# Softmax attention in a four-block network: row maxima of four heads turned and copied together

## The reference

```python
q = embedded @ Wq.T + bq; k = ...; v = ...          # 16 heads of 8 features
qk = jnp.einsum('bhqd,bhkd->bhqk', q, k) / sqrt(s)
p = jax.nn.softmax(qk, axis=-1)                      # over all 1024 keys
p = p * jnp.triu(ones((s, s)))                       # mask after the softmax
z = jnp.einsum('bhqk,bhkd->bhqd', p, v)
out = layernorm(embedded + z) * gamma + beta
```

## Time and profile before

| | us |
|---|---|
| median of 3 runs | 989.38 (987.41 to 995.13) |
| span of the profiled execution | 985.3 |
| soft stage, from the first A to the last B | 430 to 859 of the span |

### The profile page before, as it was taken

One profiled execution on the slowest core, in us unless ns is written; L12 is line 12 of the kernel. 1 busy time (PEld: TensorE's weight loads), 2 busy tenths in 40 slices (PEclk: granted clock), 3 DMA queues, 4 the chain that ended last, 5 costly groups with the idle time before them and its releaser, 6 DMA issues.

```text
span 985.3 us, 13757 instructions
## 1 busy us (share of the span) xinstructions
PE 675.3 (69%) x4446; PEld 334.1 (34%) x4446; DVE 582.2 (59%) x1035; ACT 443.7 (45%) x836; POOL 302.9 (31%) x679
## 2 busy tenths in 40 slices
PE   4042867332240992579999999999999999840694
PEld 4031322131230991213343423242323433230693
DVE  5216699760450345677878777767977777062243
ACT  2021500011210652405878676766667777720462
POOL 0605154414425341003242323141322323105242
PEclk9996889555655896757999999998999999965697
DMA  9942000002213101560030202030020000000203
GB/s 232 274 144 40 1 1 0 0 9 60 71 17 90 30 27 44 123 147 7 1 50 2 50 1 50 1 48 4 11 40 2 1 2 1 1 1 33 81 26 96
DMA packets 45926, 44.89 MB, mean 46 GB/s; under 512 B 5904, under 2 KB 36316, under 8 KB 45600
## 3 DMA queue, kind: packets, MB, share of 16 engines
q1 hardware_dynamic: 41168, 35.90, 15.6%
q0 software_dynamic: 4544, 7.60, 2.9%
q10 hardware_dynamic: 144, 0.51, 0.2%
HBM read 27.85 MB, written 17.60 MB: 46 GB/s over the span
## 4 chain that ended last, share of the span: by engine, by line
PE 51%; DVE 11%; issue 5%; DMA 5%; POOL 5%; ACT 3%; SPq 1%; POOLq 0%; ACTq 0%; DVEq 0%
PE PS L828 14%; PE PS L795 12%; PE PS L770 11%; PE PS L629 5%; PE PS L640 4%; POOL slots_x L1395 3%; DVE ARENA L1348 3%; ACT ARENA L987 2%; DMA ARENA<-slots_x 1%; POOL ARENA L1409 1%; DVE XN L1042 1%; PE PS L536 1%; DMA ARENA<-k_parts 1%; DVE STATS L1019 1%; DVE X L1086 1%
## 5 line engine op out<-in xcount | busy, mean ns | idle before, releaser
L1348 DVE TENSOR_REDUCE ARENA<-PS 128x1 f32<-128x1024 f32 x256 | 302.9, 1219 | 94.6 <-PE PS L770 94.1
L987 ACT ACTIVATE ARENA<-PS 128x512 f32<-128x512 f32 x512 | 279.6, 597 | 95.6 <-PE PS L795 89.2
L795 PE MATMUL PS<-ARENA 75*128 75x512 bf16 x512 | 174.9, 388 | 8.3 <-ACT ARENA L987 6.8
L770 PE MATMUL PS<-ARENA 72*128 72x512 bf16 x512 | 164.3, 406 | 21.3 <-DMA ARENA<-k_parts 16.9
L828 PE MATMUL PS<-ARENA 128*8 128x128 f32 (+8 forms) x1920 | 153.4, 435 | 0.7 <-ACT ARENA L987 0.7
L1460 POOL TENSOR_SCALAR_AFFINE_SELECT ARENA<-ARENA 128x128 f32<-128x128 f32 x256 | 74.6, 296 | 160.5 <-ACT ARENA L987 160.3
L581 PE MATMUL PS<-C,ARENA 128*128 128x128 f32 x78 | 17.1, 368 | 119.5 <-DMA ARENA<-slots_x 119.5
L1272 DVE TENSOR_TENSOR ARENA<-PS,ARENA 128x512 f32<-128x512 f32 x46 | 31.8, 692 | 96.3 <-PE PS L629 96.3
L554 PE MATMUL PS<-C,XN 128*128 128x128 f32 x96 | 24.1, 401 | 92.4 <-DVE XN L1042 88.8
L795 PEld LDWEIGHTS PS<-ARENA 75*128 75x128 bf16 x512 | 47.5, 98 | 105.5 <-ACT ARENA L987 56.5
L770 PEld LDWEIGHTS PS<-ARENA 72*128 72x128 bf16 x512 | 44.8, 100 | 104.1 <-issue 37.3
(11 more groups left out here) (130 smaller groups left out, 785.0 us busy)
## 6 DMA issues: line engine op xcount, KB each, us to landing
ARENA<-q_parts SPq DMA_DIRECT2D x24, 192.0 KB
ARENA<-k_parts SPq DMA_DIRECT2D x72, 64.0 KB
ARENA<-pack_dram SPq DMA_DIRECT2D x8, 514.0 KB
slots_x<-FILL SPq DMA_DIRECT2D x2, 1483.5 KB, 19.0
ARENA<-slots_x SPq DMA_DIRECT2D x10, 258.0 KB, 4.4
ARENA<-slots_x SPq DMA_DIRECT2D x8, 256.0 KB, 3.6
slots_y<-ARENA SPq DMA_DIRECT2D x16, 128.0 KB, 1.8
ARENA<-tokens_y SPq DMA_DIRECT2D x8, 256.0 KB, 3.7
```

What stands on the lines that cost most here:

```text
L770: ins = nc.tensor.matmul(PS[:, slot + c, :], Q3[0:KQ, G % Q3R, g, i * P:(i + 1) * P], K3[0:KQ, G % Q3R, g, c * 512:(c + 1) * 512], start=T ...
L795: nc.tensor.matmul(PS[:, bank, 0:w], K3[0:MR + 3, G % Q3R, i, j * P:(j + 1) * P], Q3[0:MR + 3, G % Q3R, i, half * 512:half * 512 + w], sta ...
L987: nc.scalar.activation(PT[:, n % NPT, 0:w], PS[:, 4 + ring_number[x] % NBB, 0:w], ACT.Exp).then_inc(b_exp, 1)
L1348: nc.vector.tensor_reduce(NM[:, k % 4, i:i + 1], PS[:, slot:slot + 2, :].rearrange("p b n -> p (b n)"), AX.X, ALU.max, negate=True).then_i ...
```

## The change

The unit of the maxima becomes one half of all four heads. The buffers `NM`, `NMR`, `M3` and `MT` hold 16 maxima columns (48 after the split) for each half, in two buffers where there were four. S, M and the copy are done once per half for four heads: 16 of each where there were 64. SP still issues 64 stores of the same size, now four behind each copy. PE waits at the first B of a half for all four (`m_rows[half]`, 64 counts per group). The planner's `LEAD` goes from 0 to 3: at a half's first B, three more turns must lie ahead beyond the M.

```diff
-LEAD = 0
+LEAD = 3
+MW = 4 * HQ
...
-        last = (hh, h)
+        last = (hh // 4, h) if hh % 4 == 3 else None
...
-    ahead = turns.index(("M", 3, 0)) + 1 + LEAD
+    ahead = turns.index(("M", 0, 0)) + 1 + LEAD
...
-                want = max(want, turns.index(("M", 4 * G + 3, s // TB)) + 1 + LEAD)
+                want = max(want, turns.index(("M", G, s // TB)) + 1 + LEAD)
...
-                        sp.wait_ge(m_copied, maxima_number[hh, h] + 1)
-                        sp.dma_start(Q3[MR:MR + 3, G % Q3R, g, tiles[0] * P:(tiles[-1] + 1) * P],
-                                     MT[0:3 * len(tiles), hh % 4, :]).then_inc(m_rows[hh % 4], 16)
+                        sp.wait_ge(m_copied, maxima_number[G, h] + 1)
+                        for g in range(4):
+                            sp.dma_start(Q3[MR:MR + 3, G % Q3R, g, tiles[0] * P:(tiles[-1] + 1) * P],
+                                         MT[3 * HQ * g:3 * HQ * (g + 1), h, :]).then_inc(m_rows[h], 16)
...
-                        at, width = unit_columns(i)
-                        o = PS[0:width, bank, 0:P // 2].bitcast(BF16)
-                        nc.tensor.transpose(o, M3[:, k % 4, at:at + width], IDB[:, :]).then_inc(m_turned, 1)
+                        o = PS[0:3 * MW, bank, 0:P // 2].bitcast(BF16)
+                        nc.tensor.transpose(o, M3[:, i, :], IDB[:, :]).then_inc(m_turned, 1)
...
-                            pe.wait_ge(m_rows[i], rows_stored(4 * G + i, half))
+                            pe.wait_ge(m_rows[half], 64 * (G + 1))
...
-                        nc.scalar.copy(MT[0:width, k % 4, :],
-                                       PS[0:width, 4 + ring_number[x] % NBB, 0:P // 2].bitcast(BF16)
+                        nc.scalar.copy(MT[0:3 * MW, i, :],
+                                       PS[0:3 * MW, 4 + ring_number[x] % NBB, 0:P // 2].bitcast(BF16)
                                        ).then_inc(m_copied, 1)
...
-                        nm, rest = NM[:, k % 4, tiles[0]:tiles[-1] + 1], NMR[:, k % 4, tiles[0]:tiles[-1] + 1]
-                        m0, m1, m2 = (M3[:, k % 4, at + r * n:at + (r + 1) * n] for r in range(3))
+                        nm, rest = (a[:, i, :].rearrange("p (g n) -> p g n", g=4) for a in (NM, NMR))
+                        m0, m1, m2 = (M3[:, i, :].rearrange("p (g r n) -> p g r n", g=4, r=3)[:, :, r, :]
+                                      for r in range(3))
```

More of the change, by code:

```diff
@@ L163, in macaron_kernel @@
         FILL = sb("FILL", [P, P + 1])
-        MT = sb("MT", [P, 4, P], BF16)
+        MT = sb("MT", [P, 2, P], BF16)
         B2 = sb("B2", [P, E * P])
@@ L252, in macaron_kernel @@
         ONE8 = m(32)
-        NM = m(4 * TB).rearrange("p (r i) -> p r i", r=4)
-        NMR = m(4 * TB).rearrange("p (r i) -> p r i", r=4)
-        M3 = m.bf(4 * 3 * TB).rearrange("p (r c) -> p r c", r=4)
+        NM = m(2 * MW).rearrange("p (r c) -> p r c", r=2)
+        NMR = m(2 * MW).rearrange("p (r c) -> p r c", r=2)
+        M3 = m.bf(2 * 3 * MW).rearrange("p (r c) -> p r c", r=2)
         RD = m(32).rearrange("p (c g) -> p c g", g=4)
@@ L355, in macaron_kernel @@
         m_copied = sem("m_copied")
-        m_rows = [sem(f"m_rows{k}") for k in range(4)]
+        m_rows = [sem(f"m_rows{k}") for k in range(2)]
         b_scores = sem("b_scores")
@@ L395, in macaron_kernel @@
         last_scores = {}
[L396 to L405, removed]
+        for G, h in maxima:
+            last_scores[G, h] = score_number["A", 4 * G + 3, tiles_of_unit(h)[-1]]
         turn_number = {x: n for n, x in enumerate(turns)}
@@ L413, in columns @@
             return 4 * P, (P * (j - HQ) if j >= HQ else None)
-        def unit_columns(h):
-            return 3 * HQ * h, 3 * HQ
         def masked_before(m):
@@ L500, in soft @@
                     if x[0] == "M":
-                        _, hh, h = x
-                        G, g = divmod(hh, 4)
+                        _, G, h = x
                         tiles = tiles_of_unit(h)
-                        sp.wait_ge(m_copied, maxima_number[hh, h] + 1)
-                        sp.dma_start(Q3[MR:MR + 3, G % Q3R, g, tiles[0] * P:(tiles[-1] + 1) * P],
-                                     MT[0:3 * len(tiles), hh % 4, :]).then_inc(m_rows[hh % 4], 16)
+                        sp.wait_ge(m_copied, maxima_number[G, h] + 1)
+                        for g in range(4):
+                            sp.dma_start(Q3[MR:MR + 3, G % Q3R, g, tiles[0] * P:(tiles[-1] + 1) * P],
+                                         MT[3 * HQ * g:3 * HQ * (g + 1), h, :]).then_inc(m_rows[h], 16)
                     if x[0] == "V" and x[1] % NS == NS - 1:
@@ L965, in soft @@
                         act.wait_ge(m_turned, maxima_number[k, i] + 1)
[L966 to L969, removed]
-                        nc.scalar.copy(MT[0:width, k % 4, :],
-                                       PS[0:width, 4 + ring_number[x] % NBB, 0:P // 2].bitcast(BF16)
+                        if k >= 1:
+                            act.wait_ge(m_rows[i], 64 * k)
+                        nc.scalar.copy(MT[0:3 * MW, i, :],
+                                       PS[0:3 * MW, 4 + ring_number[x] % NBB, 0:P // 2].bitcast(BF16)
                                        ).then_inc(m_copied, 1)
@@ L1344, in soft @@
                         dve.wait_ge(a_scores, score_number[x] + 1)
-                        if k >= 4 and i == 0:
-                            dve.wait_ge(m_split, last_unit(k - 4) + 1)
-                        nc.vector.tensor_reduce(NM[:, k % 4, i:i + 1],
+                        G, g = divmod(k, 4)
+                        h, it = divmod(i, HQ)
+                        if G >= 1 and g == 0 and it == 0:
+                            dve.wait_ge(m_split, maxima_number[G - 1, h] + 1)
+                        nc.vector.tensor_reduce(NM[:, h, HQ * g + it:HQ * g + it + 1],
                                                 PS[:, slot:slot + 2, :].rearrange("p b n -> p (b n)"),
@@ L1443, in soft @@
                         pool.wait_ge(a_max, last_scores[k, i] + 1)
[L1444 to L1447, removed]
-                        nm, rest = NM[:, k % 4, tiles[0]:tiles[-1] + 1], NMR[:, k % 4, tiles[0]:tiles[-1] + 1]
-                        m0, m1, m2 = (M3[:, k % 4, at + r * n:at + (r + 1) * n] for r in range(3))
+                        if k >= 1:
+                            pool.wait_ge(m_turned, maxima_number[k - 1, i] + 1)
+                        nm, rest = (a[:, i, :].rearrange("p (g n) -> p g n", g=4) for a in (NM, NMR))
+                        m0, m1, m2 = (M3[:, i, :].rearrange("p (g r n) -> p g r n", g=4, r=3)[:, :, r, :]
+                                      for r in range(3))
                         then(nc.gpsimd.tensor_copy(m0, nm))
```

## The result

The changed kernel took 1046.37 us (median of 4 runs, 1040.83 to 1056.52) against 988.39 us for the kernel before, a ratio of 1.057 with a 95% interval of 1.053 to 1.061. The forecast was 1039 in a range of 1012 to 1058. The ratio leaves out the run of 1056.52 us, which stands over 1.5% above the fastest of the four. The profiled execution has a span of 1039.1 us, 53.8 more than before. It was the fastest of the four, with the highest mean granted clock (0.816; the others had 0.797 to 0.804), so its trace shows somewhat less than the median run lost.

What follows compares the result with a forecast made beforehand. PE was taken as the bound from the first B on. At full clock 2.3 - 7.0 + 29.6 + 5 = +30 us, plus 20 for the clock, gave a span of 1035.3 and a median of 1039, range 1012 to 1058.

Steps and rivals of the forecast that it cites:

- PE is the bound from the first B on: Soft stage: PE busy 92.45 of 92.60 us, so work taken from PE shortens it and standing is lost in full.
- the sum had 7.0: Transposes M on PE: 64 become 16, their cost falling from 10.2 to 3.2 us, so -7.0 us.
- The bound of 4.7 us for the ring of banks: Second B behind M waits for an exponential at 12 places; 4.7 us at most to gain, none taken in the sum.
- The beginning, +2.3: Ahead of the first B: it comes 3.6 us later, while three A of 0.43 are missing later; +2.3 us.
- The chain of 4.7 us: At each half, from M over copy and four stores in a row to the first B: 0.54 + 2.2 + 1.92 us.
- The waits, +29.6 and +5: PE standing at the first B in halves 3 to 15, +29.6 us, and slower steps behind those waits, +5 us.
- the +5 for the steps without A: First steps behind the wait in 13 halves run at ACT's pace: 0.2 to 0.6 us each, bounds 0 and 9.
- The clock, +20: Granted clock falls to half behind the waits of halves 8 to 15, 2.5 us each: +20 us, bounds 0 and 44.
- The clock that stays up: Rival: PE keeps the full clock since A go by in the heap at each half; 1019 us, chance 0.16.
- Overlapping issues: Rival: four stores issued 0.34 us apart, chain 3.5 us; 1004, or some 1016 with clock falls at half the places; chance 0.16.

Runs made afterwards that it cites:

- e9: e5 with M held back to the next V, the last M moved to step 117, and each head waiting for its own store: 972.38 us, ratio 0.984.
- e10: e9, but the first B of a half waits for all four stores: 987.58 us, ratio 1.000.
- e5: The changed kernel with an even planner order, two A placed in each step, S and M behind theirs: 985.92 us, ratio 1.001.
- e6: The kernel before, maxima by head, with the same even planner order as e5: 993.96 us, ratio 1.010.
- e1: The changed kernel with the stores of heads 2 and 3 issued from ACT, two per queue: 1029.97 us, ratio 1.044.
- e2: The changed kernel with a semaphore for each head, so the first B waits only for head 0's store: 1027.22 us, ratio 1.041.
- e4: The kernel before with LEAD = 3 alone, maxima by head as before: 1005.74 us, ratio 1.021.
- e8: The changed kernel with LEAD = 0, the grouping without the lead: 1087.39 us, ratio 1.104.
- e3: The changed kernel with useless matmuls in halves 8 to 14, 5, 5, 5 and 6 per half: 1036.58 us, ratio 1.051.
- e7: As e3, with fewer useless matmuls, 3, 3, 3 and 2 per half: 1030.07 us, ratio 1.050.

## Why the prediction was right, point by point

- *PE is the bound from the first B on.* Right: a microsecond in which PE stood was a microsecond lost (e9 against e10: 9.7 us longer standing, 9.1 us longer stage), and less M on PE was a gain (e5 against e6: 48 M fewer, 8 us less in the medians and 6.5 in the stage of the traces, where the sum had 7.0). The bound of 4.7 us for the ring of banks was too large: the trace before has 8 such places and not 12, which makes 3.0 us.
- *The beginning, +2.3.* The first B came 2.8 us later (450.6 against 447.8), where I had 3.6: M itself came 1.0 us earlier (445.78), and the first B 4.85 behind it. Less the 1.3 us for the three A moved, that is +1.5.
- *The chain of 4.7 us.* Right: 4.65 to 5.0 us from M to the first B in halves 8 and 10 to 15, with 0.74 between issues. Half 9 took 6.84, since ACT's copy stood behind the layer-norm work, which I had left out. In halves 1 and 2 the chain was hidden, as forecast (first B 6.2 and 5.8 us behind M, no wait).
- *The waits, +29.6 and +5.* PE stood 28.1 us longer, 15.9 of it for the rows and 14.1 for DVE between the heaped A, less 1.9 elsewhere. The two terms were 6.5 us too large together. The waits for ACT didn't grow (6.4 against 6.8), so the +5 for the steps without A isn't seen as standing; those steps ran mostly at half clock, so what they would cost at the full clock isn't shown. The waits as I listed them add up to 31.1 with a chain of 4.7 and not to 30.3, a slip that changes nothing.
- *The clock, +20.* This term was somewhat too small, and its reason was in part wrong. Nine falls were seen, eight of them where I had put them (halves 8 to 15), and one at half 4. But they lasted 7.9 us on average, not the 3.4 to 6.8 I took from before. In the nine stretches PE was busy 62.0 us, in the two before 10.0; at half clock half of that is loss, 26 us of busy time more than before, as an estimate. Waits, clock, transposes and the A moved to the beginning make 28.1 + 26 - 7.0 - 1.3 = 46 of the 50.5 us by which the stage from first to last B grew; 4.7 us I can't assign. By the price of the two pairs above it is 21 to 23 us. As the reason I had named the long waits at each half, 2.9 to 3.1 us. But e1 and e2 cut the wait for the rows from 16.6 to 5.3 and 3.6 us and the falls stayed (75.0 and 78.5 us), and e4 has falls with no wait for rows at all. Falls came with the short stops of a heap and with long waits without a heap (e8) alike; waits of 0.3 to 0.9 us before the first B of each half, without a heap (e10), came with a single fall. What exactly sets off a fall stays open.
- *The span and the median.* The span was forecast at 1035.3 and was 1039.1. The median stood 7.3 us above it, where before it was 4.1; the runs of the changed kernel also spread wider, and the longer ones have the lower clock. That the forecast came so near is partly luck: the terms for the waits were 6.5 us too large, while the clock's term and the part that I can't assign left out some 11.
- *The rivals.* The clock that stays up is out (nine falls, and e3 and e7 show that they cost time). Overlapping issues are out by the row of 2.92 us for four. By the Trainium skill, "DMA: Bandwidth & Descriptors", section "Anatomy of one DMA — SWDGE (gpsimd) path", most of a DMA's fixed cost of about 2 us is the wait for completion and not setup, by which four stores would cost hardly more than one; e1 and e2 show that the row of four costs 13 to 15 us here. The 2 us did hold for the last one of a row: from the first issue to the first B are 4.14 us at half 12, less three issues of 0.74 leaves 1.92.

What the experiments add: the grouping isn't bad in every plan. The lead alone costs 20 us, the grouping without a lead 102; together they cost 58, and with M two steps ahead in an even order the grouping is a gain of 8 over its like with 64 transposes, and level with the kernel before.

## What to carry to other kernels

When small transfers are gathered into one point, ask what starts behind the last of them: a row of issues on one queue is a chain of its own length, and the first consumer should wait only for its own. Producers belong a fixed distance ahead of the deadline, in an even row; a planner that catches up at the deadline puts its heap exactly where PE has nothing else. And where PE is full, stops are often paid twice, once as the stop and once in the clock: here 28 us of longer standing came with 61 us more at half clock, and shortening the longest of the waits didn't bring the clock back. So look at the granted clock and at PE's busy time beside its waits.

## What the runs showed of the hardware that wasn't expected

- A store from SBUF to SBUF of 12 rows of 256 bytes holds the issuing queue for 0.7 us or more, on SP and on ACT alike (1.44 and 1.56 us for two), where three loads of 64 KB are issued in 0.99 us.
- The granted clock fell at the end of a heap in which PE never stood longer than 1.6 us at a time (half 11: 0.61, 0.53 and 1.61 us), and stayed at half for 13.7 us, though PE was busy for 13.15 of them.
- The same order with the same waits can keep the full clock in one execution and lose it in another (half 4: 28.98 us in e7, 31.55 in the changed kernel).
- An M of 48 rows takes PE hardly longer by its own row than one of 12 (0.24 against 0.22 us), but behind a V it puts off the next matmul by 0.15 to 0.17 us where one of 12 did by 0.03; ACT's copy of it takes 0.25 against 0.24 us in the median.
